# First attention: GpSimd takes the first maxima earlier, and VectorE finishes the layer norm and writes two groups' rows

## The chip, the cores and the metric

The kernel runs on one core of a Trainium2 chip. The metric is the device time of one execution in microseconds (us), the median of several executions; lower is better. The core's engines each work through a queue of their own in order and meet at semaphores: TensorE (PE, matmuls and transposes), VectorE (DVE), ScalarE (ACT), GpSimd (POOL) and SyncE (SP, which here issues the loads).

## The reference

The input x is 16 x 256 tokens of 128 numbers. Four layers follow one another, each with a cross attention onto a context of 64 tokens and a feed-forward part, each behind a layer norm without weights and with a residual sum. The change touches the first attention alone:

```python
def _layernorm(x, axis=-1, eps=1e-05):
    m = jnp.mean(x, axis=axis, keepdims=True)
    v = jnp.var(x, axis=axis, keepdims=True)
    return (x - m) / jnp.sqrt(v + eps)

# _L0_xattn_ref(x, context, mask, Wq, Wkv, Wo): 2 heads of 64
    q = (x @ Wq).reshape(B, N, H, D).transpose(0, 2, 1, 3)
    kv = (context @ Wkv).reshape(B, M, 2, H, D).transpose(2, 0, 3, 1, 4)
    k, v = (kv[0], kv[1])
    attn = jnp.einsum('bhnd,bhmd->bhnm', q, k) * SCALE
    attn = jnp.where(mask[:, None, :, :], attn, -jnp.inf)
    attn = jax.nn.softmax(attn, axis=-1)
    out = jnp.einsum('bhnm,bhmd->bhnd', attn, v)
    out = out.transpose(0, 2, 1, 3).reshape(B, N, C)
    return out @ Wo

    x = x + _L0_xattn_ref(_layernorm(x, axis=-1), ctx_1024, mask_BxSxS2_bf1, ...)
    x = x + _L0_ffn_ref(_layernorm(x, axis=-1), ...)      # quantised: needs maxima over all tokens
```

## The kernel before

The 4096 tokens stay in SBUF as 32 tiles of 128 tokens (X), and the work goes in eight groups of four tiles (512 tokens). All engines' queues are written out by hand, one function for each engine and stage: `att0_pe`, `att0_act`, `att0_dve` and `att0_pool` are the first attention. Nothing else sets the order; a semaphore count in front of an instruction is its only tie to the others.

One group g passes through these steps, named as in the code:

- **Rows** (`normalise` on VectorE, L325, or `norm` on GpSimd, L1180): four instructions write (x - mean) * rstd into `hrow`, which has two places, for even and odd groups. They need the layer norm of their tiles.
- **T(g)** on TensorE (L336) transposes the rows, and ScalarE copies them out (`take_turned`, L341).
- **Q(g)** (L935) is the query product; `takeQ` on ScalarE (L1046, L1049) copies it twice, in bf16 and in f32.
- **MX(g)** (L945, L947) forms the scores in bf16 with the mask added; `mx(g)` on VectorE (L1097) takes each row's negated maximum.
- **less_max(g)** on GpSimd (L1171) adds the negated maximum to the mask.
- **ST(g)** (L960, L962) forms the scores transposed, mask and maximum included. It also waits for the values, since its first use of PSUM bank 3 comes behind V(3), which ScalarE's `values(3)` (L1038) must have copied out. `exp(g)` (L1055) is its exponential.
- **PV(g)** (L972) multiplies by the values, **over(g)** on VectorE (L1105, L1109) divides by the sums, **TO(g)** (L983) transposes, `take_out` (L1061) copies, **O(g)** (L991) is the output product, and `add` (L1115) adds it to X. `tail_stats` (L357, L360) takes the statistics for the next part.

TensorE's order in iteration i is ST(i), Q(i+2), MX(i+1), PV(i), O(i-1), T(i+3), TO(i). Ahead of the loop stand K, V, T(0) to T(2), Q(0), Q(1) and MX(0). In three of the iterations VectorE also quantises the weights of the feed-forward part (`f0_weights_dve`, L1202 to L1208).

The layer norm of x has two parts: tiles 0 to 11 (groups 0 to 2), and tiles 12 to 31, which arrive with a later load. Each part is statistics on VectorE (`first_stats`, L1120), six small instructions (`ln_var_dve`, L224 to L232), a logarithm and an exponential on ScalarE (`ln_finish_act`, L307 and L311), and four small instructions on VectorE (`ln_rstd_dve`, L243 to L249).

GpSimd begins by converting the mask (uint8) into bf16 numbers to add, in eight instructions of two groups' half each (L1161).

Of the kernel before, what the change touches and what calls it, by code (L numbers as in the profile page):

```python
# [32 lines left out]
N_GROUPS = N_TILES // 4  # L33
# [45 lines left out]
def build(nc, dram):  # L79
    with ExitStack() as ctx:  # L80
# [111 lines left out]
        def sem(s, name):  # L192
            return S("all_" + name)

        def at(s, name):
            return sum(count(x, name) for x in SUB[:SUB.index(s)])
# [100 lines left out]
        def ln_finish_dve(dve, s, k=0):  # L297
            ln_var_dve(dve, s, k)
            ln_rstd_dve(dve, s, k)

        def ln_finish_act(act, s, k=0):

            lo, hi = ln_parts(s)[k]
            if s in ("a0", "a1") and k == 0:
                act.preload_act_table_set("natural_log_exp_and_others")
            act.wait_ge(sem(s, "var"), at(s, "var") + k + 1)
            act.activation(lnw[:, 5, lo:hi], lnw[:, 4, lo:hi], ACT.Ln).then_inc(S("all_lnv"), 1)  # L307
            act.wait_ge(S("all_lnv"), at(s, "var") + k + 1)
            if s == "f2" and k == 1:
                act.activation(late_y, lnw[:, 5, lo:hi], ACT.Exp, scale=-0.5)  # L310
            act.activation(lnw[:, 6, lo:hi], lnw[:, 5, lo:hi], ACT.Exp, scale=-0.5).then_inc(sem(s, "std"), 1)  # L311
# [713 lines left out]
        def att0_act(act):  # L1025
            s = "a0"

            def keys(i):
                act.wait_ge(hs("k_ps"), i + 1)
                for h in range(2):  # L1030
                    act.activation(kbd[:, 8 * i:8 * i + 8, h * SK:(h + 1) * SK],
                                   bank(3 + i).rearrange("p (b k) -> p b k", k=SK), ACT.Copy,
                                   scale=W["kmask64"][:, h:h + 1]).then_inc(hs("k"), 1)

            def values(i):
                act.wait_ge(hs("v_ps"), i + 1)
                for h in range(2):
                    act.activation(vw0[:, 4 * i:4 * i + 4, h, 0:64],  # L1038
                                   bank(5 + i if i < 3 else 3).rearrange("p (b n) -> p b n", b=4)[:, :, h * 64:(h + 1) * 64],
                                   ACT.Copy, scale=W["kmask64"][:, h:h + 1]).then_inc(hs("v"), 1)  # L1040

            def takeQ(g):
                act.wait_ge(hs("q_ps"), g + 1)
                if g >= 2:
                    act.wait_ge(hs("mx_ps"), g - 1)
                act.activation(q16_0[g % 2], bank(1), ACT.Copy).then_inc(hs("q16"), 1)  # L1046
                if g >= 3:
                    act.wait_ge(hs("st_ps"), g - 2)
                act.activation(qT0[g % 3], bank(1), ACT.Copy).then_inc(hs("qT"), 1)  # L1049

            def exp(g):
                act.wait_ge(hs("st_ps"), g + 1)
                if g >= 2:
                    act.wait_ge(hs("pv"), g - 1)
                act.activation(pt0[g % 2], bank(3), ACT.Exp, scale=64 ** -0.5).then_inc(hs("pt"), 1)  # L1055

            def take_out(g):
                act.wait_ge(hs("to"), g + 1)
                if g >= 2:
                    act.wait_ge(hs("o_ps"), g - 1)  # L1060
                act.activation(oT0[g % 2], bank(4), ACT.Copy).then_inc(hs("oT"), 1)  # L1061

            keys(0)
            keys(1)
            values(0)
            values(1)
            take_turned(act, s, 0, 0)
            takeQ(0)
            values(2)
            take_turned(act, s, 1, 1)  # L1070
            takeQ(1)
            values(3)
            take_turned(act, s, 2, 0)
            for i in range(N_GROUPS):
                exp(i)
                if i + 2 < N_GROUPS:
                    takeQ(i + 2)
                if i == 0:
                    ln_finish_act(act, s, 1)
                if i + 3 < N_GROUPS:  # L1080
                    take_turned(act, s, i + 3, (i + 3) % 2)
                take_out(i)
            f0_weights_act(act)

        def att0_dve(dve, nxt):
            s = "a0"
            dve.sem_inc(sem(s, "res"), 1)

            def keys16(i):
                dve.wait_ge(hs("k"), 2 * i + 2)  # L1090
                dve.tensor_copy(kbd16[:, 8 * i:8 * i + 8, :], kbd[:, 8 * i:8 * i + 8, :]).then_inc(hs("kb"), 1)

            def mx(g):
                dve.wait_ge(hs("mx_ps"), g + 1)
                if g >= 2:
                    dve.wait_ge(hs("kv"), g - 1)
                dve.tensor_reduce(nm0[g % 2], bank(2).rearrange("p (h k) -> p h k", k=SK), AX.X, ALU.max,  # L1097
                                  negate=True).then_inc(hs("mx"), 1)

            def over(g):  # L1100

                dve.wait_ge(hs("pv"), g + 1)
                both = psum[:, 5:7, 0:260].rearrange("p c (t n) -> p c t n", n=65)
                rz = rz0[g % 2].rearrange("p (c t) -> p c t", c=2)
                dve.reciprocal(rz, both[:, :, :, 64]).then_inc(hs("rz"), 1)  # L1105
                dve.wait_ge(hs("rz"), g + 1)
                if g >= 2:
                    dve.wait_ge(hs("to"), g - 1)
                dve.tensor_tensor(ow0[g % 2].rearrange("p (c t n) -> p c t n", c=2, t=4), both[:, :, :, 0:64],  # L1109
                                  rz.unsqueeze(3).to_broadcast([P, 2, 4, 64]), ALU.mult).then_inc(hs("ow"), 1)  # L1110

            def add(g):
                dve.wait_ge(hs("o_ps"), g + 1)
                xg = X[:, 4 * g:4 * g + 4, :]
                dve.tensor_tensor(xg, xg, bank(7).rearrange("p (t n) -> p t n", t=GT), ALU.add)\  # L1115
                    .then_inc(sem(s, "res"), 1)

            def first_stats(lo, hi):
                for t in range(lo, hi):
                    dve.bn_stats(stats[:, t, :], X[:, t, :]).then_inc(S("bn0"), 1)  # L1120

            normalise(dve, s, 0, 0)
            keys16(0)
            normalise(dve, s, 1, 1)
            dve.wait_ge(S("ld_x"), 32)
            first_stats(LN0, LN0 + 8)
            mx(0)
            normalise(dve, s, 2, 0)
            keys16(1)
            first_stats(LN0 + 8, N_TILES)  # L1130
            mx(1)
            dve.wait_ge(S("bn0"), N_TILES)
            dve.sem_inc(sem(s, "stats"), 1)
            ln_finish_dve(dve, s, 1)
            for i in range(N_GROUPS):
                if i and i + 1 < N_GROUPS:
                    mx(i + 1)
                over(i)
                if i:
                    add(i - 1)  # L1140
                    tail_stats(dve, s, i - 1, False)
                if 3 <= i < 6:
                    f0_weights_dve(dve, i - 3)
            rows_dve(dve)
            add(N_GROUPS - 1)
            tail_stats(dve, s, N_GROUPS - 1, False)
            stats_done(dve, s, nxt)
            dve.sem_inc(S("f0_go"), 1)

        def att0_pool(pool):  # L1150
# [5 lines left out]
                .then_inc(S("f3_pad"), 1)  # L1156
            pool.tensor_copy(vw0[:, :, :, 64], W["kmask64"].unsqueeze(1).to_broadcast([P, B, 2])).then_inc(hs("ones"), 1)
            pool.wait_ge(S("ld_mask"), 16)
            for c in range(4):
                for h in range(2):  # L1160
                    pool.tensor_scalar(m16[:, 8 * c:8 * c + 8, h * SK:(h + 1) * SK],  # L1161
                                       mask_u8[:, 8 * c * SK:8 * (c + 1) * SK].rearrange("p (t k) -> p t k", k=SK),
                                       1.0, MASKED, ALU.subtract, ALU.mult).then_inc(hs("mask"), 1)
# [9 lines left out]
                                   nm0[g % 2].unsqueeze(2).to_broadcast([P, 8, SK]), ALU.add).then_inc(hs("kv"), 1)  # L1173

            def norm(g):
                if g == 3:
                    pool.wait_ge(sem(s, "ln"), 2 * LN_STEPS)
                pool.wait_ge(sem(s, "turned"), at(s, "turned") + g + 1)
                for t in range(GT):
                    ins = pool.tensor_scalar(hrow[:, g % 2, t * P:(t + 1) * P], X[:, 4 * g + t, :],  # L1180
                                             mean[:, 4 * g + t:4 * g + t + 1], rstd[:, 4 * g + t:4 * g + t + 1],
                                             ALU.subtract, ALU.mult)
                ins.then_inc(sem(s, "normed"), 1)

            for g in range(N_GROUPS):
                less_max(g)
                if g + 3 < N_GROUPS:
                    norm(g + 3)
# [1775 lines left out]
```

## Time and profile before

| | |
|---|---|
| median of 3 runs | 1173.81 us (1173.71 to 1174.62) |
| profiled execution | 1166.1 us |
| its span | 1164.3 us |
| mean granted TensorE clock | 0.915 |
| TensorE busy | 937.1 us (80%) |
| VectorE busy | 831.0 us (71%) |
| ScalarE busy | 647.7 us (56%) |
| GpSimd busy | 470.9 us (40%) |

The span runs from the first to the last recorded instruction. The profiled execution took 1.8 us more than its span. It is also 7.7 us shorter than the median of the runs without a profile. The first attention lies in the first 84 us of the span.

### The profile page before, as it was taken

What the parts mean: (1) busy time and instruction counts of PE and PEld (TensorE: products, weight loads), DVE (VectorE), ACT (ScalarE), POOL (GpSimd) and SP (SyncE); (2) the same over time, 40 slices, a digit from 0 to 9 for tenths busy, and PEclk for the clock granted to TensorE, in tenths of its full rate; (3) what the DMA queues carried; (4) which work ended last, traced back from release to release, by engine and by line L of the source; (5) the groups of instructions that cost most, each with busy time, mean ns of one, the idle gap of its engine ahead of it and who ended that gap; (6) DMA issues with size and microseconds to landing.
All of it is one profiled execution on the core that took longest, in us unless ns stands there. A gap on an engine that the chain in (4) does not pass through costs nothing.

```text
span 1164.3 us, 21022 instructions
## 1 busy us (share of the span) xinstructions
PE 937.1 (80%) x7158; PEld 629.4 (54%) x7158; DVE 831.0 (71%) x2070; ACT 647.7 (56%) x1143; POOL 470.9 (40%) x454
## 2 busy tenths in 40 slices
PE   4877820378997999689858999998988987957997
PEld 2663310364545677345434766665654545536896
DVE  5596689876887675467787999999857886622443
ACT  3423567956653345556547878775635655213554
POOL 6610000001220001435368999999311224473555
PEclk9998975588999999899987999999878998987999
DMA  8000000028000000000000000000000000024431
GB/s 288 1 1 1 0 1 0 0 71 273 2 1 1 1 1 2 1 2 1 2 1 1 1 0 0 0 0 1 1 1 1 2 2 1 24 105 116 113 104 34
DMA packets 24233, 33.76 MB, mean 29 GB/s; under 512 B 3484, under 2 KB 20389, under 8 KB 23888
## 3 DMA queue, kind: packets, MB, share of 16 engines
q1 hardware_dynamic: 20720, 26.20, 7.4%
q0 software_dynamic: 3424, 6.38, 1.6%
q8 instruction: 55, 0.90, 0.3%
q14 instruction: 34, 0.28, 0.1%
HBM read 18.34 MB, written 15.98 MB: 29 GB/s over the span
## 4 chain that ended last, share of the span: by engine, by line
PE 33%; DVE 28%; issue 9%; ACT 5%; POOL 3%; DVEq 0%; DMA 0%; POOLq 0%; ACTq 0%; SPq 0%
DVE hq L845 7%; DVE big L850 7%; PE psum L619 5%; PE psum L2523 5%; PE psum L1591 3%; POOL rows L2393 3%; ACT psum L2034 2%; DVE big L2182 2%; PE psum L2539 2%; PE psum L573 2%; PE psum L1608 2%; DVE big L854 2%; DVE psum L1839 1%; DVE tmp L1827 1%; DVE psum L1827 1%
## 5 line engine op out<-in xcount | busy, mean ns | idle before, releaser
L845 DVE TENSOR_REDUCE hq<-psum 128x16 f32<-128x1024 f32 x96 | 114.4, 1220 | 81.2 <-PE psum L573 44.2
L2105 POOL TENSOR_TENSOR big<-big 128x512 f32<-128x512 f32 x128 | 128.7, 1050 | 7.0 <-ACT big L1867 7.0
L2182 DVE SCALAR_TENSOR_TENSOR big<-big,tmp,psum 128x512 f32<-128x512 f32 x128 | 90.4, 744 | 7.6 <-ACT psum L2034 4.7
L2034 ACT ACTIVATE psum<-big,tmp 128x512 f32<-128x512 f32 x128 | 84.9, 686 | 19.3 <-DVE big L2182 16.7
L735 ACT ACTIVATE big<-psum 128x1024 f32<-128x1024 f32 x64 | 62.0, 1021 | 54.5 <-PE psum L603 54.5
L850 DVE RECIPROCAL big<-psum 128x256 f32<-128x256 f32 x48 | 84.0, 1750 | 5.6 <-PE psum L619 5.4
L2710 DVE SCALAR_TENSOR_TENSOR big<-psum,big 128x128 f32<-128x128 f32 x118 | 36.0, 347 | 72.5 <-issue 44.2
L483 POOL TENSOR_TENSOR big<-big,w_const 128x256 f32<-128x256 f32 x32 | 23.3, 728 | 150.3 <-PE psum L619 143.2
L2115 POOL TENSOR_TENSOR big<-big 128x1024 f32<-128x1024 f32 x32 | 75.4, 2366 | 15.8 <-DVE big L2182 15.8
L1505 PE MATMUL psum<-f_downT,tmp 128*128 128x128 f32 x192 | 25.7, 300 | 68.0 <-DVE tmp L1388 68.0
L2403 POOL DMA_INDIRECT out<-big x59 | 57.9, 982 | 50.5 <-issue 30.3
L619 PE MATMUL psum<-big 128*32 128x256 f32 x768 | 52.3, 388 | 26.0 <-DVE big L854 23.9
L1274 DVE TENSOR_REDUCE amax<-big 128x1 f32<-128x1536 f32 x32 | 55.9, 1748 | 22.5 <-ACT big L1414 22.5
L599 PE MATMUL psum<-hq,big 32*128 32x256 f32 x768 | 65.5, 428 | 6.1 <-DVE hq L845 5.9
L341 ACT ACTIVATE hT<-psum 128x512 f32<-128x512 f32 x56 | 33.3, 595 | 61.5 <-PE psum L336 61.5
L2523 PE MATMUL psum<-tmp,big 128*128 x236 | 63.1, 391 | 0.0
L1505 PEld LDWEIGHTS psum<-f_downT,tmp 128*128 128x128 f32 x192 | 25.3, 216 | 68.8 <-DVE tmp L1388 68.3
L1247 POOL PARTITION_ALL_REDUCE qs<-qs x4 | 1.5, 371 | 145.8 <-DVEq L1227 132.2
L491 POOL TENSOR_TENSOR big<-big,w_a 128x256 f32<-128x256 f32 x16 | 11.6, 728 | 119.3 <-ACT big L707 119.3
L336 PE MATMUL psum<-w_const,hrow 128*128 128x128 f32 x224 | 37.8, 295 | 24.5 <-DVE hrow L1298 10.7
L483 POOL TENSOR_TENSOR big<-w_f,w_const 128x256 f32<-128x256 f32 x16 | 12.6, 792 | 108.3 <-PE psum L619 85.4
L619 PE MATMUL psum<-big,w_const 128*32 128x256 f32 x768 | 52.2, 389 | 0.0
(334 smaller groups left out, 2621.4 us busy)
## 6 DMA issues: line engine op xcount, KB each, us to landing
rows<-pad SPq DMA_DIRECT2D x1, 7670.0 KB, 33.0
big<-rows SPq DMA_DIRECT2D x59, 130.0 KB
tmp<-in_pack_f SPq DMA_DIRECT2D x1, 2050.5 KB, 9.7
w_f<-in_pack_f SPq DMA_DIRECT2D x1, 1280.0 KB, 12.6
tmp<-in_pack_once SPq DMA_DIRECT2D x1, 960.0 KB, 7.1
out<-big POOLq DMA_INDIRECT x59
X<-in_x SPq DMA_DIRECT2D x1, 768.0 KB, 5.6
w_a<-in_pack_a SPq DMA_DIRECT2D x3, 256.0 KB, 8.0
```

The source lines that it names most:

```text
L599: pe.matmul(bank(1 + r)[:, 256 * e:256 * e + 256], L.kbd[rows, b, e * P:(e + 1) * P], L.qT[b % L.ahead][rows, :], start=True, stop=False)
L619: ins = pe.matmul(bank(6)[32 * r:32 * r + 32, 256 * which:256 * which + 256], w, L.pt[b % 2][:, (2 * r + e) * 256:(2 * r + e + 1) * 256], ...
L735: act.activation(L.pt[b % 2][:, 1024 * half:1024 * half + 1024], psum[:, 1 + 2 * half:3 + 2 * half, :].rearrange("p c n -> p (c n)"), ACT.Exp,
L845: dve.tensor_reduce(nm, psum[:, 1 + 2 * t:3 + 2 * t, :].rearrange("p c (r l k) -> p (c r) l k", r=2, k=SK), AX.X, ALU.max, negate=True).th ...
L850: dve.reciprocal(L.rz, bank(6)[:, 256:512]).then_inc(hs("rz"), 1)
L1274: dve.tensor_reduce(amax[:, i, g:g + 1], A[:, g, :], AX.X, ALU.max, apply_absolute_value=True).then_inc(S("f0_am"), 1)
L2034: act.activation(bank(EX_BANK + h % 2), ssum[t][:, h * 512:(h + 1) * 512], ACT.Exp, bias=shift2[:, t * NH2 + h:t * NH2 + h + 1]).then_inc( ...
L2105: ins = pool.tensor_tensor(ssum[t][:, h * 512:(h + 1) * 512].rearrange("p (i j) -> p i j", i=ROWS2), st[:, 0, h, 0:ROWS2].unsqueeze(2).to_ ...
L2115: pool.tensor_tensor(ew[t][:, 0:left], ew[t][:, 0:left], ew[t][:, NFOLD * 512:], ALU.add)\
L2182: dve.scalar_tensor_tensor(out=ew[t][:, blk], in0=ssum[t][:, blk], scalar=best2[:, t, h, 7:8], in1=bank(EX_BANK + h % 2), op0=ALU.is_ge, o ...
L2403: pool.indirect_dma_start(dram["out"], bass.IndirectOffsetOnAxis(slot3[j % RS][:, ID3:ID3 + 1].bitcast(U32), 0), out3[j % RS], None, bound ...
L2523: ins = pe.matmul(bank(2 + j % 2)[:, 2 * P * k:2 * P * (k + 1)], hTb[j % 3], W["f3_w"][:, ds(weights_at(j, k), 2 * P)], start=True, stop=True)
```

## The change

- GpSimd: the eight mask conversions are cut into a helper `masks(lo, hi)`, and `less_max(0)` stands behind the fifth of them, `less_max(1)` behind the seventh.
- GpSimd no longer writes the rows of groups 3 and 4. VectorE does, with `normalise`. GpSimd's first `norm` is that of group 5, which also waits until VectorE's rows are counted.
- VectorE: the second part of the layer norm stands right behind its statistics, ahead of `mx(1)`; behind it come the rows of group 3, `mx(1)`, and the rows of group 4.
- ScalarE: the logarithm and the exponential of the second part stand ahead of `takeQ(2)`, not behind it.

```diff
@@ att0_act
             for i in range(N_GROUPS):
                 exp(i)
+                if i == 0:
+                    ln_finish_act(act, s, 1)
                 if i + 2 < N_GROUPS:
                     takeQ(i + 2)
-                if i == 0:
-                    ln_finish_act(act, s, 1)
@@ att0_dve
             first_stats(LN0 + 8, N_TILES)
-            mx(1)
             dve.wait_ge(S("bn0"), N_TILES)
             dve.sem_inc(sem(s, "stats"), 1)
             ln_finish_dve(dve, s, 1)
+            normalise(dve, s, 3, 1)
+            mx(1)
+            normalise(dve, s, 4, 0)
@@ att0_pool
-            for c in range(4):
-                for h in range(2):
+
+            def masks(lo, hi):
+
+                for i in range(lo, hi):
+                    c, h = divmod(i, 2)
                     pool.tensor_scalar(m16[:, 8 * c:8 * c + 8, h * SK:(h + 1) * SK],
...
             def norm(g):
-                if g == 3:
+                if g == 5:
                     pool.wait_ge(sem(s, "ln"), 2 * LN_STEPS)
+                    pool.wait_ge(sem(s, "normed"), at(s, "normed") + 5)
...
-            for g in range(N_GROUPS):
+            masks(0, 5)
+            less_max(0)
+            masks(5, 7)
+            less_max(1)
+            masks(7, 8)
+            for g in range(2, N_GROUPS):
                 less_max(g)
                 if g + 3 < N_GROUPS:
                     norm(g + 3)
```

GpSimd's queue in the first attention, before. L1161 is a mask conversion, L1171 is `less_max`, and four of L1180 are one group's rows:

```order
L1161 TENSOR_SCALAR big<-mask_u 128x8x64 x8
L1171 TENSOR_TENSOR big<-big 128x512
L1180 TENSOR_SCALAR hrow<-X,lnw 128x128 x4
L1171 TENSOR_TENSOR big<-big 128x512
L1180 TENSOR_SCALAR hrow<-X,lnw 128x128 x4
L1171 TENSOR_TENSOR big<-big 128x512
```

The same place of the changed kernel, where the conversions have line L1166, `less_max` L1176 and the rows L1186:

```order
L1166 TENSOR_SCALAR big<-mask_u 128x8x64 [waits ld_mask]
L1166 TENSOR_SCALAR big<-mask_u 128x8x64 x4
L1176 TENSOR_TENSOR big<-big 128x512 [waits att_mask,att_mx]
L1166 TENSOR_SCALAR big<-mask_u 128x8x64 x2
L1176 TENSOR_TENSOR big<-big 128x512 [waits att_mx]
L1166 TENSOR_SCALAR big<-mask_u 128x8x64
L1176 TENSOR_TENSOR big<-big 128x512 [waits att_mask,att_st_ps,att_mx]
L1186 TENSOR_SCALAR hrow<-X,lnw 128x128 [waits all_turned,all_normed,all_ln]
```

Two groups' rows have gone, the first `less_max` stands ahead of three conversions, and the second ahead of one.

VectorE's queue from the last of the first statistics (L1120), before. L1097 is `mx(1)` and L1105 begins `over(0)`:

```order
L1120 BN_STATS stats<-X 128x6 x12
L1097 TENSOR_REDUCE big<-psum 128x8 [waits att_mx_ps]
L224 TENSOR_TENSOR lnw<-stats 128x20 [waits bn0,all_stats]
...
L249 SCALAR_TENSOR_TENSOR lnw<-lnw 128x20 [waits all_ln]
L1105 RECIPROCAL big<-psum 128x8 [waits att_pv,all_ln]
L1109 TENSOR_TENSOR big<-psum,big 128x512 [waits att_rz]
```

The same place of the changed kernel:

```order
L1120 BN_STATS stats<-X 128x6 x12
L224 TENSOR_TENSOR lnw<-stats 128x20 [waits bn0,all_stats]
...
L249 SCALAR_TENSOR_TENSOR lnw<-lnw 128x20 [waits all_ln]
L325 TENSOR_SCALAR hrow<-X,lnw 128x128 [waits all_turned,all_ln]
L325 TENSOR_SCALAR hrow<-X,lnw 128x128 x3
L1097 TENSOR_REDUCE big<-psum 128x8 [waits att_mx_ps]
L325 TENSOR_SCALAR hrow<-X,lnw 128x128 [waits all_turned]
L325 TENSOR_SCALAR hrow<-X,lnw 128x128 x3
L1105 RECIPROCAL big<-psum 128x8 [waits att_pv]
```

`mx(1)` has gone behind the layer norm and the rows of group 3, and `over(0)` behind the rows of group 4 (L325). TensorE's queue is unchanged.

## Rows read from the trace of the kernel before

**Rows 1.** The page, part 4: the chain that ended last, by engine.

```profile
PE 33%; DVE 28%; issue 9%; ACT 5%; POOL 3%; DVEq 0%; DMA 0%; POOLq 0%; ACTq 0%; SPq 0%
```

**Rows 2.** Timeline, TensorE: start, duration, engine, line, operation, tiles, count [idle before, releaser].

```profile
26.92 1.22 PE L960 MATMUL psum<-big 128*128 128x256 f32 x2 [4.47 <-POOL big L1171]
...
37.24 1.11 PE L336 MATMUL psum<-w_const,hrow 128*128 128x128 f32 x4 [5.11 <-POOL hrow L1180]
38.15 1.06 PE L983 MATMUL psum<-w_const,big 128*128 128x128 f32 x4
...
44.38 0.60 PE L983 MATMUL psum<-w_const,big 128*128 128x128 f32 x4
44.82 0.60 PE L960 MATMUL psum<-big 128*128 128x256 f32 x2
...
47.33 1.11 PE L972 MATMUL psum<-big 128*128 128x130 f32 x8
...
50.04 0.60 PE L960 MATMUL psum<-big 128*128 128x256 f32 x2
```

**Rows 3.** Timeline, GpSimd, the first 40 us.

```profile
9.51 16.23 POOL L1161 TENSOR_SCALAR big<-mask_u 128x512 bf16<-128x512 uint8 x8 [1.15 <-DMA mask_u<-in_mask]
25.82 1.04 POOL L1171 TENSOR_TENSOR big<-big 128x512 bf16<-128x512 bf16 x1
34.06 3.12 POOL L1180 TENSOR_SCALAR hrow<-X,lnw 128x128 f32<-128x128 f32 x4 [7.19 <-DVE lnw L249]
```

**Rows 4.** Timeline, ScalarE, around the first scores and in the steady part.

```profile
21.91 0.84 ACT L1038 ACTIVATE big<-psum,w_const 128x256 f32<-128x256 f32 x2
...
29.57 0.60 ACT L1055 ACTIVATE big<-psum 128x512 f32<-128x512 f32 x1 [6.33 <-PE psum L962]
...
46.17 0.60 ACT L1055 ACTIVATE big<-psum 128x512 f32<-128x512 f32 x1 [0.50 <-PE psum L962]
```

**Rows 5.** Timeline, VectorE, from the third group's rows to the first division.

```profile
19.28 1.40 DVE L325 TENSOR_SCALAR hrow<-X,lnw 128x128 f32<-128x128 f32 x4
...
21.20 2.41 DVE L1120 BATCH_NORM_STATS2 stats<-X 128x6 f32<-128x128 f32 x12
31.21 0.69 DVE L1097 TENSOR_REDUCE big<-psum 128x8 f32<-128x512 f32 x1 [7.61 <-PE psum L947]
31.82 0.18 DVE L224 TENSOR_TENSOR lnw<-stats 128x20 f32<-128x20 f32 x1
...
33.05 0.18 DVE L243 TENSOR_TENSOR lnw<-lnw 128x20 f32<-128x20 f32 x1 [0.54 <-ACT lnw L311]
...
33.98 0.21 DVE L1105 RECIPROCAL big<-psum 128x8 f32<-128x8 f32 x1
34.22 0.69 DVE L1109 TENSOR_TENSOR big<-psum,big 128x512 f32<-128x512 f32 x1
```

**Rows 6.** Windows: stretch, length, each engine's busy time (count), granted clock, DMA share, GB/s.

```profile
24.00:26.00 2.00, 0.00 (x0) 0.00 (x0) 0.00 (x0) 0.00 (x0) 1.92 (x2) 1.00 0.93 389
26.00:28.00 2.00, 1.08 (x3) 0.72 (x4) 0.00 (x0) 0.00 (x0) 0.87 (x1) 0.64 0.18 70
...
36.00:38.00 2.00, 0.76 (x4) 0.76 (x5) 0.00 (x0) 0.00 (x0) 2.00 (x3) 0.70 0.00 0
...
40.00:42.00 2.00, 2.00 (x16) 1.28 (x15) 0.00 (x0) 0.74 (x2) 1.29 (x2) 0.94 0.00 0
...
60.00:64.00 4.00, 3.24 (x25) 2.17 (x23) 3.93 (x11) 2.07 (x4) 1.04 (x1) 1.00 0.01 2
...
84.00:88.00 4.00, 3.21 (x17) 3.00 (x16) 2.51 (x16) 0.46 (x2) 0.38 (x1) 0.57 0.01 2
```

**Rows 7.** Timeline, TensorE, behind the last output product of this attention.

```profile
83.19 0.91 PE L2764 MATMUL psum<-w_a,bvmat 128*128 128x128 f32 x6 [2.55 <-DVEq L1148]
```

**Rows 8.** One line's instructions: operation, count, durations in ns (least, median, most).

```profile
L325 DVE TENSOR_SCALAR hrow<-X,lnw x12: 334/453/703, 12.6 to 20.3; 128x128 f32<-128x128 f32 x12
```

**Rows 9.** Timeline, VectorE: the next layer norm's first instruction.

```profile
83.97 0.20 DVE L224 TENSOR_TENSOR lnw<-stats 128x32 f32<-128x32 f32 x1
```

## The prediction, made before the changed kernel had run

> **What bounds the kernel now.** I read the page first. The last chain runs over TensorE and VectorE for 61% of the span, GpSimd has 3% [rows 1], so GpSimd matters only where the others stand still for it. I then read TensorE's timeline of the first 50 us for gaps. There are two. ST(0) starts at 26.92, released by GpSimd's `less_max(0)`, after 4.47 us idle, so T(2) ahead of it ended at 22.45. Behind PV(0) TensorE is idle again for 5.11 us, until T(3) at 37.24, which waits for group 3's rows from GpSimd [rows 2]. From ST(2) on it has no gap: ST(2) to ST(3) is 44.82 to 50.04, so 5.22 us a group, bound by TensorE [rows 2]. Where VectorE quantises the weights, it is the bound: 3.93 us busy of the 4 from 60 to 64 [rows 6]. At 83.97 the next layer norm begins [rows 9]. Each stage behind needs the one ahead, and the only other outside dates are the loads, which are over early: the DMA share is 0.18 at 26 to 28 us and 0.00 behind it [rows 6]. So whatever ST(2) gains, the end should gain. The question is when ST(2) starts; before it is 44.82.
>
> GpSimd's timeline shows both gaps' causes. Eight conversions take 9.51 to 25.74, then `less_max(0)` 1.04. Then GpSimd idles 7.19 us for the layer norm, and the rows take 3.12 [rows 3]. The layer norm's second part starts at 31.82 although its statistics end at 23.61, since `mx(1)` stands ahead and waits 7.61 us for MX(1), which is behind ST(0) on TensorE [rows 5].
>
> **First gap: ST(0).** Five conversions at 16.23 / 8 = 2.03 us end at 9.51 + 10.1 = 19.7, and with 1.04 `less_max(0)` is done at 20.7. `mx(0)`, which it needs, stands ahead of the rows that VectorE starts at 19.28 [rows 5], so it is no later than the fifth conversion. ST(0) is then released by something else: `values(3)` on ScalarE ends at 21.91 + 0.84 = 22.75 [rows 4]. I put ST(0) at 22.82 instead of 26.92. That is 4.10 us. The two conversions behind it end at 20.7 + 4.06 = 24.8 and wait for nobody.
>
> ST(0) also runs faster. In the stretch 24 to 26 us, with TensorE idle, the granted clock is still 1.00 (2.4 GHz). In 26 to 28 it is 0.64 on average, so it fell to 0.50 (1.2 GHz) at about 26.6, and ST(0) runs at that [rows 6]. At full clock ST(i) to `exp(i)` is 44.82 to 46.17, 1.35 us, against 26.92 to 29.57, 2.65, at half [rows 2, 4]. So `exp(0)` starts at 24.17 and ends at 24.77. Before it was 29.57 to 30.17.
>
> **Second gap: T(3) and TO(0).** VectorE goes on from 23.61 with `ln_var`. Before, it took from 31.82 until the wait of 0.54 ahead of L243 at 33.05 began, 0.69 us, so it is ready at 24.3. ScalarE has the logarithm behind `exp(0)` and starts it at 24.77; with the 0.54 that the two functions cost VectorE [rows 5], L243 starts at 25.3. From L243 to the next part's first instruction is 33.05 to 33.98, 0.93: `normalise(3)` starts at 26.25. On ScalarE, `takeQ(2)` comes about 0.5 us later for the move; its copies are next needed by MX(2) and ST(2), far off.
>
> The nearest row for one group's rows on VectorE is 1.40 us for the four at 19.28 [rows 5]. I take it for both groups; by the least and the median of twelve it would be 4 x 0.334 = 1.3 and 4 x 0.453 = 1.8 [rows 8]. So group 3's rows are there at 27.65 and T(3) can start. `mx(1)` (0.69, of which some 0.6 before the next can start) ends at 28.3, the rows of group 4 at 29.7. `over(0)` from its start to its end is 33.98 to 34.91, 0.93, so 30.6. TO(0) starts at 30.65, not 38.15. This is the new last wait. PV ends 3.62 us behind the start of its ST (44.82 to 47.33 + 1.11), so PV(0) ends at 26.4, and TensorE's gaps are now about 1.3 us ahead of T(3) and, T(3) being 0.5 long, 2.4 us between T(3) and TO(0). The eight row instructions add 2.8 us to VectorE, and what is queued behind them is `over(0)`, for which TO(0) and with it all of TensorE waits. That is the price of the move, and it is inside the sum. GpSimd gives 2 x 3.12 us back, most of it idle time anyway.
>
> Who else could be late? `less_max(1)` runs 28.3 to 29.4, ST(1) needs it at 31. The last conversion ends at 31.4. `less_max(2)` waits for `mx(2)`, which follows MX(2), right ahead of PV(1): 2.51 us behind ST(1) (44.82 to 47.33 [rows 2]) and 0.69 for itself, so 34.3. `norm(5)` then ends at 34.3 + 1.04 + 3.12 = 38.5, and T(5) stands 0.9 us ahead of ST(3) at 41.5, so at 40.6. All are hidden, with 1.6, 2.9 and 2.1 us to spare.
>
> **The sum.** At full clock TO(0) takes 0.44 (44.38 to 44.82) [rows 2], ST(1) starts at 31.1 and ST(2) 5.22 later at 36.3. Before: 44.82. Gain 8.5 us.
>
> **The clock.** Less is left if the granted clock falls in the two new gaps. The trace has a fall after a shorter idle time than the two large ones: TensorE idles 2.55 us ahead of L2764 and works again from 83.19, and yet the clock of 84 to 88 is 0.57 [rows 6, 7]. The new gaps are 1.3 and 2.4 us with one 0.5 us transposition between. I choose the fall. How long half clock then lasted is in the means of two stretches: 0.70 in 36 to 38 is a fall at 36.8, and 0.94 in 40 to 42 a return at 40.25 [rows 6], 3.4 us. Work at half clock takes about twice as long (TO(0) lasts 1.06 at 38.15 against 0.60 at 44.38, with its fixed start [rows 2]), so if it falls just ahead of TO(0), 1.7 us of TensorE's work is lost, and if some of it passes in the gap, 1.2. I take 1.4. Gain 8.5 - 1.4 = 7.1 us.
>
> On the profiled execution's own time, 1166.1 - 7.1 = 1159.0 us. The runs' median is 7.7 us above that execution, in which nothing here tells why; I carry the difference over: 1173.8 - 7.1 = **1166.7 us**.
>
> **Rivals.**
> Clock stays full through the gaps: gain 8.5, 1165.3 us. For it: with ST(0) to PV(0) at full speed just before, neither new gap is as long as the 2.55 us ahead of L2764. Against it: the fall at 84 us.
>
> VectorE's rows wait for GpSimd. The mechanism would be that `normalise(4)`, which starts in the same moment as `less_max(1)`, waits for it (1.04) and, losing once more, for the last conversion (1.92). `over(0)` and all behind it come up to 3.0 later: gain 7.1 - 3.0 = 4.1, 1169.7 us. Against it: the twelve row instructions of groups 0 to 2 ran beside conversions that went on without a break, and the longest took 0.703 us [rows 3, 8]. The Trainium skill, SBUF — State Buffer, section on who interferes with whom, says just this: a VectorE tensor_scalar in a two-port mode and a GpSimd instruction lock each other out, and the second to issue blocks fully until the first is done. By that rule instructions among those twelve should have stood for up to a whole conversion, and the time would be this rival's 1169.7. None did, so the trace does not bear it out here.
>
> Hidden anyway: something behind takes the gain back, for instance the weights' load or a date in the next part. The loads are over by 28 us [rows 6], so I know of no such date. 1173.8 us.
>
> Slower: the clock stays at half when the steady part begins. A group there is TensorE work without a gap; were its steps to double nearly all, 5.22 would become about 9.4 us (estimated as 5.22 x 1.8, from TO's 1.06 against 0.60), 4.2 more for each group. Two groups use the gain up; over four groups it is 7.1 - 16.8 = 9.7 us slower, 1183.5 us. For it: at 84 us the clock fell under a working TensorE. Against it: behind both large gaps it came back, the second time after 3.4 us, once gap-free work ran [rows 6].
>
> That the change doesn't do what it says I rule out: the queues show `less_max(0)` behind the fifth conversion.
>
> **How the numbers follow.** Forecast (clock falls, gain about 7): 0.50; its own range is 1166.3 to 1168, from the 1.7 and 1.2 of the clock and 0.8 for slower rows. Clock stays: 0.27. Rows wait for GpSimd: 0.08. A smaller gain of 2 to 5 from a wait I haven't seen: 0.07. Hidden: 0.03. Slower: 0.05. This kernel's measurement tells about 0.2% (2.3 us) from no change. So faster 0.91, same 0.04, slower 0.05. Range: below, the full gain 8.5, with 1.7 us more if the runs' own two clock dips cost more than the profiled one's, 1163.5; above, the GpSimd rival, 1170.0.
>
> **What would show it.** In the changed profile: ST(0) (L960) at 22.8, released by ScalarE's L1038 and not by GpSimd; layer norm L243 at 25.3; L325 eight more times, of which the last ends near 29.7; TO(0) (L983) at 30.6 released by VectorE's L1109; ST(2) at 37.7 (36.3 with a full clock); the next layer norm at about 77 instead of 83.97. The windows from 30 to 34 us tell whether the clock fell. The forecast is wrong if `over(0)` ends past 32, if GpSimd's L1176 releases ST(1), or if the first attention is 7 us shorter and the total is not.

## The result, and the profile after

The changed kernel took 1170.16 us (median of 7 runs, 1169.31 to 1172.08), the kernel before, run beside it, 1174.26. The ratio is 0.9957, 95% interval 0.9937 to 0.9978, so by the ratio it is 5.0 us faster (2.6 to 7.4); the two medians lie 4.1 us apart. The forecast was 7.1 us, 1166.7; the median lies 0.2 us above the range that was given, with a kernel before that ran 0.5 us longer than in the runs at hand then. Two later repetitions gave ratios of 0.9959 and 0.9976 (below). So the direction was right and the size too large by 2 to 4 us.

TensorE's timeline of the profile after, to be laid beside [rows 2]. This execution ran 0.63 us ahead of the first from the start: T(2) starts at 21.16 instead of 21.79. That is not the change's work: e4 below, whose code is the same up to there, has T(2) at 21.88.

```profile
21.16 0.66 PE L336 MATMUL psum<-w_const,hrow 128*128 128x128 f32 x4
22.25 0.67 PE L960 MATMUL psum<-big 128*128 128x256 f32 x2 [0.43 <-ACT big L1038]
...
27.52 0.66 PE L336 MATMUL psum<-w_const,hrow 128*128 128x128 f32 x4 [1.58 <-DVE hrow L325]
31.14 1.11 PE L983 MATMUL psum<-w_const,big 128*128 128x128 f32 x4 [2.96 <-DVE big L1109]
32.05 1.06 PE L960 MATMUL psum<-big 128*128 128x256 f32 x2
...
39.01 0.60 PE L960 MATMUL psum<-big 128*128 128x256 f32 x2
```

These rows show the two gaps and what ends them. ST(0) is released by ScalarE's values after 0.43 us, no longer by GpSimd after 4.47. T(3) comes 9.7 us earlier by the clock of the trace. But TO(0) waits 2.96 us for VectorE's division, TO(0) to ST(1) takes 0.91 us, which is half clock, and ST(1) to ST(2) takes 6.96 instead of the 5.22 of a full-clock group. With the 0.63 us added, TO(0) stands at 31.77 (forecast 30.65) and ST(2) at 39.64 (forecast 37.7). The gain at ST(2) is 44.82 - 39.64 = 5.2 us.

VectorE's timeline, to be laid beside [rows 5], shows why TO(0) waited:

```profile
18.63 2.47 DVE L325 TENSOR_SCALAR hrow<-X,lnw 128x128 f32<-128x128 f32 x4
...
21.63 2.40 DVE L1120 BATCH_NORM_STATS2 stats<-X 128x6 f32<-128x128 f32 x12
24.19 0.19 DVE L224 TENSOR_TENSOR lnw<-stats 128x20 f32<-128x20 f32 x1 [0.15 <-DVEq L1132]
...
25.42 0.18 DVE L243 TENSOR_TENSOR lnw<-lnw 128x20 f32<-128x20 f32 x1 [0.54 <-ACT lnw L311]
...
26.35 1.12 DVE L325 TENSOR_SCALAR hrow<-X,lnw 128x128 f32<-128x128 f32 x4
27.38 0.69 DVE L1097 TENSOR_REDUCE big<-psum 128x8 f32<-128x512 f32 x1
27.98 2.26 DVE L325 TENSOR_SCALAR hrow<-X,lnw 128x128 f32<-128x128 f32 x4
30.17 0.19 DVE L1105 RECIPROCAL big<-psum 128x8 f32<-128x8 f32 x1
```

One group's rows take 1.12 us (group 3) and 2.26 (group 4), and group 2's, whose code the change does not touch, 2.47 instead of 1.40. GpSimd's timeline beside it:

```profile
19.29 1.04 POOL L1176 TENSOR_TENSOR big<-big 128x512 bf16<-128x512 bf16 x1
20.42 3.93 POOL L1166 TENSOR_SCALAR big<-mask_u 128x512 bf16<-128x512 uint8 x2
28.15 1.07 POOL L1176 TENSOR_TENSOR big<-big 128x512 bf16<-128x512 bf16 x1 [3.81 <-DVE big L1097]
29.30 1.92 POOL L1166 TENSOR_SCALAR big<-mask_u 128x512 bf16<-128x512 uint8 x1
```

Both slow groups have a `less_max` beside them, at 19.29 and at 28.15, and the conversion that follows it. Looked at one by one, the rows hold an instruction that lasts far longer than the 0.703 us of [rows 8] (columns as there):

```profile
L325 DVE TENSOR_SCALAR hrow<-X,lnw x20: 332/472/1140, 12.3 to 29.9; 128x128 f32<-128x128 f32 x20
```

The windows, to be laid beside [rows 6], show the clock:

```profile
28.00:30.00 2.00, 0.18 (x2) 0.00 (x0) 2.00 (x5) 0.60 (x1) 1.76 (x2) 0.69 0.03 8
30.00:32.00 2.00, 0.86 (x4) 0.86 (x5) 1.05 (x3) 0.00 (x0) 1.22 (x1) 0.50 0.00 0
32.00:34.00 2.00, 2.00 (x8) 1.34 (x7) 0.00 (x0) 0.60 (x1) 0.00 (x0) 0.50 0.00 0
34.00:36.00 2.00, 2.00 (x8) 0.96 (x7) 0.00 (x0) 0.60 (x1) 0.00 (x0) 0.60 0.00 0
```

A mean of 0.69 is a fall from full clock (2.4 GHz) to half (1.2 GHz) at 28.8, and one of 0.60 a return at 35.6. It stayed at half for 6.8 us, 4.5 of them with TensorE at work, not for 3.4.

The next layer norm begins at 78.16 instead of 83.97 [rows 9]: what was gained at ST(2), 5.8 us by the trace's clock (5.2 without the earlier start), came through the rest of the first attention whole.

```profile
78.16 0.20 DVE L224 TENSOR_TENSOR lnw<-stats 128x32 f32<-128x32 f32 x1
```

Yet this execution took 1169.6 us, 3.5 more than the profiled one of before. In the last stage both VectorE and ScalarE stand still for some 12 us, with no releaser that the profile knows ("remote"), as the waits of the kernel after say (engine, line, releaser: total, times, longest):

```profile
DVE big L2655 <- remote: 15.1, 2, 11.5
ACT big L2559 <- remote: 12.2, 1, 12.2
```

### The profile page after: what moved, and what is told of

Read it like the earlier page. It is cut to its first block, busy times and chain, and to the rows that moved or that the text cites. A ratio compares the mean times of both kernels' runs of the same rounds, so it can differ in the third digit from the quotient of the medians.

```text
span 1167.8 us, 21022 instructions
## 1 busy us (share of the span) xinstructions
PE 939.7 (80%) x7158; PEld 630.9 (54%) x7158; DVE 836.0 (72%) x2078; ACT 647.1 (55%) x1143; POOL 464.6 (40%) x446
## 4 chain that ended last, share of the span: by engine, by line
PE 35%; DVE 29%; issue 8%; ACT 5%; another core or an unknown queue 1%; POOL 1%; DVEq 1%; DMA 0%; POOLq 0%; ACTq 0%; SPq 0%
DVE big L850 7%; DVE hq L845 7%; PE psum L619 5%; PE psum L2534 5%; PE psum L1602 3%; ACT psum L2045 2%; DVE big L2193 2%; PE psum L2550 2%; PE psum L573 2%; PE psum L1619 2%; DVE big L854 2%; DVE psum L1850 1%; DVE tmp L1838 1%; DVE psum L1838 1%; PE psum L2436 1%
## 5 line engine op out<-in xcount | busy, mean ns | idle before, releaser
L1972 PEld LDWEIGHTS psum<-w_const,big 128*128 128x128 f32 x384 | 47.3, 196 | 8.6 <-issue 8.6
```

## The experiments

Each was timed in rounds beside the kernel before, on the same chip: e1 to e4 on one chip, e5 to e8 on another, e9 and e10 later on that second one. The kernel before had a median of 1167 to 1168 us in all three sets, about 6 less than in the first comparison. Runs of different sets are compared by their ratios.

| run | median us | ratio, 95% interval | gain us |
|---|---|---|---|
| e1, before again | 1167.13 | 0.9997 (0.9983 to 1.0011) | 0.4 |
| e2, first maxima early alone | 1163.59 | 0.9959 (0.9943 to 0.9975) | 4.8 |
| e3, rows and layer norm on VectorE alone | 1164.38 | 0.9971 (0.9958 to 0.9984) | 3.4 |
| e4, division ahead of group 4's rows | 1158.42 | 0.9917 (0.9901 to 0.9934) | 9.7 |
| e5, after again | 1162.76 | 0.9959 (0.9946 to 0.9973) | 4.8 |
| e6, both groups' rows ahead of mx(1) | 1160.90 | 0.9944 (0.993 to 0.9957) | 6.5 |
| e7, gap filled | 1159.26 | 0.993 (0.9917 to 0.9944) | 8.2 |
| e8, e4 with less_max kept apart | 1156.92 | 0.991 (0.9895 to 0.9925) | 10.5 |
| e9, before a third time | 1167.64 | 1.0004 (0.999 to 1.0017) | -0.5 |
| e10, after a third time | 1163.83 | 0.9976 (0.9965 to 0.9988) | 2.8 |

The gain is one minus the ratio, times the median of the kernel before beside it (1167.98, 1167.81 or 1166.86).

### Is the stop in the last stage the change's? (e1, e5, e9, e10)

The kernels are the two of the comparison, unchanged.

> The kernel before, unchanged, profiled once more. In the changed kernel's profile VectorE and ScalarE stand still for 11.5 and 12.2 us at about 1018 to 1030 us, with no releaser in the profile; the first profile of the kernel before has no such stop and is 7.7 us shorter than its timed runs. Theory A (the stop belongs to this program's usual executions, and the first profile was an exception): this profile takes 1173 to 1175 us and shows a stop of some 8 us in the last stage. Rival B (the changed kernel brings the stop): no stop here, a profiled execution of about 1166 us again. The ratio is 1.000 by both.

> The changed kernel, unchanged, beside the others of this call. Theory: it gains at ST(2) what its first profile showed, 5.2 us once the earlier start is taken off, so a ratio of 0.9955; TO(0) follows T(3) by 3.6 us with the clock at half from then on. The stop of 11.5 us of VectorE and ScalarE in the last stage of its first profile: by theory A (part of any execution now and then, of this program or of the other) it is absent or elsewhere in this profile; by rival B (a part of the changed kernel) it is there again at about 1018 us.

> The kernel before, profiled a third time. The executions timed beside the changed kernel's first profile had a median of 1174.3 us, those beside the later runs 1168. If this is the slower set again, theory A expects a stop of VectorE and ScalarE of 7 to 12 us in the last stage of this profile, at a time of about 1174 us; at a time of about 1167 us no such stop, as in the two profiles so far. Rival B expects no stop at either time.

> The changed kernel, profiled a third time beside the kernel before. In either set it is 5 us faster than that one; a stop in the last stage is in both kernels' profiles or in neither by theory A. Rows of group 4 again 2.2 to 2.3 us, TO(0) 3.6 us behind T(3).

No profile of the four has a wait on "remote". The spans are 1165.5 and 1166.4 us before, 1157.0 and 1158.2 after. So rival B has fallen in its strict form: the changed kernel runs without the stop, twice of three profiles. Theory A is not shown either, since no execution of the kernel before with a stop was caught; e1 missed the 1173 to 1175 us that it had been given. The executions that would decide it, at 1174 us, did not come again. What the rows do give is the stop's price. From the first instruction of the last layer norm to the end of the span it is 202.8 us in the profile with the stop, and 195 to 196 in each of e1 to e10. That is 7.5 us, near the 6 to 7 by which both kernels' medians lay higher in the first comparison. A stop in most executions of that comparison, of either kernel, would fit this. It is an argument only, and the first profile of before, with 192.0 us in this stretch, differs from all the others too.

The early part repeats well. In e5 T(2) starts at 21.27 and TO(0) at 31.27, group 4's rows take 2.27 us, and ST(2) starts at 39.21 against 45.19 in e1. In e10 it is 39.88 against 45.82 in e9. The next layer norm comes 5.8, 6.0 and 6.0 us earlier in the three pairs of profiles, of which 0.6, 0.5 and 0.8 are the earlier start (T(2)). The timed runs say 5.0, 4.8 and 2.8.

### The two parts alone (e2, e3)

e2 keeps the rows of groups 3 and 4 on GpSimd:

```diff
-            for c in range(4):
-                for h in range(2):
...
-            for g in range(N_GROUPS):
+            masks(0, 5)
+            less_max(0)
+            masks(5, 8)
+            norm(3)
+            less_max(1)
+            norm(4)
+            for g in range(2, N_GROUPS):
```

> One part alone: less_max(0) behind the fifth mask conversion; conversions six to eight, the rows of groups 3 and 4 on GpSimd and VectorE's and ScalarE's order as before. Theory: ST(0) starts 4.1 us earlier at full clock, and with it MX(1), mx(1), the layer norm and GpSimd's rows of group 3: by the chain MX(1), mx(1), layer norm, 3.1 us of rows, T(3) starts near 31.7 instead of 37.2 and ST(2) about 5.4 us earlier, which is as much as or more than the whole change gave at ST(2) (5.8 us with 0.6 us of it from an earlier start). So a median of 1168.5 to 1170. Rival: the rows on VectorE carry the gain, and this part alone gives 4.1 us or less, 1170 to 1172.

It gained 4.8 us. Its TensorE timeline (T(2) at 22.70, so 0.9 later from the start than in e1):

```profile
23.81 0.67 PE L960 MATMUL psum<-big 128*128 128x256 f32 x2 [0.45 <-ACT big L1038]
...
32.60 1.11 PE L336 MATMUL psum<-w_const,hrow 128*128 128x128 f32 x4 [5.10 <-POOL hrow L1183]
```

ST(0) went as expected, and T(3), less 0.9, came at 31.7. The whole first gap was saved, and the second kept its 5.1 us. ST(2) started at 41.72, which less 0.9 is 4.4 us earlier than in e1, not 5.4. What is missing is the clock's, for ST(1) to ST(2) took 7.36 us where e1 had 5.96. A mean of 0.97 in 30 to 32 us and of 0.82 in 38 to 40 is half clock from 31.9 to 38.7, 6.8 us, where e1 had 3.4 behind the same gap. The whole change gained 5.4 us at ST(2) by e5 against e1, each from its own T(2). So in the trace this part gave four fifths of the whole. The timed runs can't tell the two apart, and 4.8 us (2.9 to 6.7) does not rule out the rival's 4.1 either.

e3 is the changed kernel with all conversions first:

```diff
-            masks(0, 5)
-            less_max(0)
-            masks(5, 7)
-            less_max(1)
-            masks(7, 8)
+            masks(0, 8)
+            less_max(0)
+            less_max(1)
```

> The other part alone: VectorE's and ScalarE's order and the rows of groups 3 and 4 on VectorE as in the change, but all eight mask conversions ahead of less_max(0). Theory: ST(0) stays at 26.9 at half clock, exp(0) at 29.6; the layer norm's logarithm waits for exp(0) and comes at 30.2, so rows of group 3 at 31.7 to 32.8, rows of group 4 with no conversion beside them, over(0) ends near 35.5, TO(0) at 35.6 instead of 38.15: a gain of 2.5 us, median about 1171.7. Rival (the parts do not add up because the gap ahead of TO(0) is the same): no gain, 1174.

It gained 3.4 us (1.9 to 4.9), and TO(0) started at 35.94. The theory stands, and the rival, no gain, fell. Group 4's rows took 1.83 us, with only `less_max(1)` beside them:

```profile
33.21 1.83 DVE L325 TENSOR_SCALAR hrow<-X,lnw 128x128 f32<-128x128 f32 x4
```

At ST(2) the parts gain 4.4 and 1.9 us, 6.3 together, and the whole change 5.4. By the timed runs it is 4.8 and 3.4 against 4.8, each give or take 1.3 to 1.9 us. What is lost between them is in the new gap ahead of TO(0), which the next runs take apart.

### The gap ahead of TO(0) (e4, e6)

e4 changes two places on VectorE:

```diff
             mx(1)
+            over(0)
             normalise(dve, s, 4, 0)
...
-                over(i)
+                if i:
+                    over(i)
```

> The changed kernel with over(0) ahead of group 4's rows on VectorE. Theory (TO(0) at 31.14 waited for over(0), which stood behind rows of 2.26 us, and the clock fell in that gap of 2.96 us): TO(0) starts near 28.9, the gap ahead of it is about 0.5 us, the clock stays full, ST(2) at about 34.3 instead of 39.0: 3.5 to 4.7 us less than the changed kernel, median 1165.5 to 1167. Rival (the clock falls all the same in the gap ahead of T(3)): 2.2 us less, 1168. Rival (the next wait takes its place, less_max(1) or group 4's rows for T(4)): less than 1 us.

It gained 9.7 us, 4.9 more than e5 by the ratios. TO(0) started at 29.49 after a gap of 0.78 us, the granted clock was 1.00 in every stretch from 22 to 38, and ST(2) started at 35.20. In the trace both rivals fell: the clock did not, and the next wait came nowhere near. Group 4's rows are not wanted before T(4) at 34.33, 4.8 us behind TO(0), and they had been put ahead of the one instruction for which TensorE stood still.

e6 leaves the division last but moves both groups' rows ahead of `mx(1)`:

```diff
             normalise(dve, s, 3, 1)
-            mx(1)
             normalise(dve, s, 4, 0)
+            mx(1)
```

> The changed kernel with the rows of group 3 and of group 4 both ahead of mx(1), so that both are written while GpSimd has nothing under way. Theory (group 4's rows took 2.26 us and group 3's 1.12 because GpSimd ran less_max(1) beside the first): both take 1.1 us, over(0) starts 1.1 us earlier and TO(0) with it; 1.1 us less than the changed kernel, or about 2 less where the shorter gap spares clock. Rival (group 4's rows are slow for another reason, their place in SBUF or the load's late tiles): 2.2 us again, no gain.

VectorE's timeline of e6, with both groups in one row:

```profile
26.59 2.14 DVE L325 TENSOR_SCALAR hrow<-X,lnw 128x128 f32<-128x128 f32 x8
28.64 0.69 DVE L1097 TENSOR_REDUCE big<-psum 128x8 f32<-128x512 f32 x1
29.24 0.20 DVE L1105 RECIPROCAL big<-psum 128x8 f32<-128x8 f32 x1
```

Eight instructions take 2.14 us when GpSimd rests, so the same rows of group 4 are about 1.1 and not 2.27. It is GpSimd's work beside them that stretched them, not their place or tiles, and the rival fell. `less_max(1)` alone made them 1.83 (e3), 0.7 more; the other 0.4 came with the conversion that follows it. TO(0) came 1.05 us earlier than in e5 (30.22 against 31.27), but ST(2) only 0.5 (38.68 against 39.21): in both runs the clock's means are 0.76 in 28 to 30 and 0.53 in 34 to 36, so half clock lasted from 29.0 to 35.9 in both, and work that came earlier met more of it. By the ratios e6 gained 1.7 us more than e5, with intervals that overlap.

### What half clock cost (e7)

```diff
                 if i + 3 < N_GROUPS:
                     T(i + 3)
+                if i == 0:
+                    for t in range(20):
+                        pe.transpose(bank(7)[:, (t % 4) * P:(t % 4 + 1) * P], ident, ident)
                 TO(i)
```

> The changed kernel with 20 more transposes of the identity into a PSUM bank that nobody reads, between T(3) and TO(0), some 2.2 us at full clock in a gap of 2.96 us. Theory (the granted clock fell in this gap and half clock cost about 2 us): the clock stays at 1.00 from 28 to 38 us, ST(1) to ST(2) takes 5.22 and not 6.96 us, TO(0) 0.44 and not 0.91, and the kernel is 2.2 us faster than the changed one. Rival (the clock falls whatever fills the gap, or the gap ahead of T(3) is what makes it fall): ST(1) to ST(2) again near 6.9, the same time or, with the fillers in the way of TO(0), up to 1 us more.

TensorE's timeline of e7:

```profile
27.52 0.66 PE L336 MATMUL psum<-w_const,hrow 128*128 128x128 f32 x4 [1.60 <-DVE hrow L325]
28.01 2.35 PE L1020 MATMUL psum<-w_const 128*128 128x128 f32 x20
31.14 0.66 PE L983 MATMUL psum<-w_const,big 128*128 128x128 f32 x4 [0.79 <-DVE big L1112]
31.63 0.60 PE L960 MATMUL psum<-big 128*128 128x256 f32 x2
...
36.85 0.60 PE L960 MATMUL psum<-big 128*128 128x256 f32 x2
```

Its windows, where e5 has 0.76, 0.50, 0.50 and 0.53 in the clock's column:

```profile
28.00:30.00 2.00, 2.00 (x21) 2.00 (x20) 2.00 (x5) 0.60 (x1) 1.77 (x2) 1.00 0.00 0
30.00:32.00 2.00, 1.21 (x10) 0.90 (x9) 1.05 (x3) 0.17 (x1) 1.22 (x1) 1.00 0.00 0
32.00:34.00 2.00, 2.00 (x16) 1.22 (x14) 0.00 (x0) 1.13 (x3) 0.00 (x0) 1.00 0.00 0
34.00:36.00 2.00, 2.00 (x23) 2.00 (x21) 1.37 (x3) 0.98 (x2) 0.89 (x1) 1.00 0.00 0
```

TO(0) starts at the same time as in the first profile after, 31.14, behind the same rows of 2.27 us. With 20 transposes whose result nobody reads, the clock does not fall, TO(0) to ST(1) is 0.49 instead of 0.91, and ST(1) to ST(2) 5.22 instead of 6.96. That is 2.2 us at ST(2), as expected, and the clock's part in the first attention is shown. By the ratios e7 gained 3.4 us more than e5, and the intervals do not overlap; the 1.2 us beyond ST(2)'s are not traced. Over the whole program e7's mean granted clock was 0.914 to 0.917, e5's 0.910 to 0.914.

### less_max kept away from the rows (e8)

On top of e4's edit:

```diff
-            masks(0, 5)
+            masks(0, 6)
             less_max(0)
-            masks(5, 7)
+            masks(6, 8)
             less_max(1)
-            masks(7, 8)
```

> over(0) ahead of group 4's rows as in the run before it, and GpSimd's order changed so that less_max(0) comes behind six conversions and less_max(1) behind all eight. Theory (less_max(0) beside group 2's rows makes these 2.3 us instead of 1.4, which delays the statistics and the layer norm by about 0.6): group 2's rows take 1.4 to 1.6 us, the layer norm starts 0.6 us earlier, ST(0) is released at the same time, since six conversions and less_max(0) end at about 22.8; 0.5 us less than the run with over(0) first alone. Rival (ST(0) now waits for less_max(0)): same time or up to 0.7 us more.

VectorE's timeline of e8:

```profile
19.31 1.27 DVE L325 TENSOR_SCALAR hrow<-X,lnw 128x128 f32<-128x128 f32 x4
...
23.66 0.19 DVE L224 TENSOR_TENSOR lnw<-stats 128x20 f32<-128x20 f32 x1 [0.15 <-DVEq L1132]
...
25.34 0.18 DVE L243 TENSOR_TENSOR lnw<-lnw 128x20 f32<-128x20 f32 x1 [0.98 <-ACT lnw L311]
```

Group 2's rows are 1.27 us beside a conversion; in e4, beside `less_max(0)`, they are 2.27. The layer norm starts 1.05 us earlier than in e4 (24.71), of which 0.6 reaches L243, for the logarithm now waits behind `exp(0)` (0.98 us instead of 0.54). ST(0) is at 22.93 as in e4, and ST(2) at 34.63 instead of 35.20. The theory stands in the trace. In the time, a ratio of 0.9910 against 0.9917, the step is too small to be told. This is the fastest version, 10.5 us below the kernel before and 5.8 below the changed one.

## Why the prediction was right, and where its size was off

**The first gap** was read rightly: ST(0) released by ScalarE's values, `exp(0)` at full clock, the conversions behind it in nobody's way. This part of the edit alone (e2) gained 4.4 us at ST(2), and 4.8 in the timed runs.

**The rows on VectorE** were mis-sized, and this is the step that failed first. I took 1.40 us for each group, with 1.8 as the upper bound, from twelve instructions that ran beside conversions [rows 5, 8]. Group 3's took 1.12, group 4's 2.26: 0.6 us more for the pair. The same contention had a second effect that I did not name at all. `less_max(0)`, moved up, now lies beside the rows of group 2. They went from 1.40 to 2.47 us, and with them L243, behind the statistics and the layer norm's first instructions, from my 25.3 to 26.05 (25.42 + 0.63). Both together make TO(0) 1.1 us late.

I had weighed this as a rival, at 0.08, and set it aside, since beside GpSimd's conversions, 1.92 us long, no row instruction took longer than 0.703 us. That is true, but of conversions only. Beside a `less_max` of 1.04 us, one row instruction lasts 1.07 to 1.14 us instead of 0.34. So the rival's mechanism did come about, in the order that it gave: `less_max(1)` cost group 4's rows 0.7 us and the last conversion 0.4, 1.1 in place of its 3.0.

The Trainium skill, SBUF — State Buffer, section on who interferes with whom, says that of a VectorE tensor_scalar in a two-port mode and a GpSimd instruction the second to issue blocks fully. The measurement agrees for GpSimd's tensor_tensor (28.15 to 29.22), with the row instruction that started just behind it and ended 0.08 us after it. It disagrees for the uint8 conversion. In e9 a conversion that began at 19.45 was under way when group 2's rows started at 19.93. These took 1.10 us, as if alone; it was the conversion, the second of the two in this row, that grew from 1.92 to 2.65 us (the timeline from 19 us on):

```profile
17.45 4.65 POOL L1161 TENSOR_SCALAR big<-mask_u 128x512 bf16<-128x512 uint8 x2
19.93 1.10 DVE L325 TENSOR_SCALAR hrow<-X,lnw 128x128 f32<-128x128 f32 x4
```

I carried the row of one GpSimd instruction over to another kind, and dismissed the rule with it.

**The clock** fell, as I chose. Its cost was mis-sized: I took one stay at half clock of 3.4 us, cost 1.4; it stayed for 6.8, and TO(0) and the group behind ST(1) lost 0.5 + 1.7 = 2.2 us. e7 gives just that back at ST(2). A length read once was not enough here. The kernel before has both: its second gap, of 5.1 us, was followed by 3.4 us at half clock in its first profile and in e1, and by 6.8 in e9, in whose rows 0.71 is a fall at 34.8 and 0.58 a return at 41.7:

```profile
34.00:36.00 2.00, 0.00 (x0) 0.00 (x0) 1.26 (x4) 0.00 (x0) 1.39 (x2) 0.71 0.00 0
40.00:42.00 2.00, 2.00 (x9) 1.35 (x8) 0.00 (x0) 0.45 (x2) 1.84 (x3) 0.58 0.00 0
```

So the forecast took the shorter of two lengths as the only one. The first profile after, e5, e6 and e10 all have 6.8 us. 1.1 us from the rows and 0.8 from the clock are the 1.9 us between the forecast and the measured ST(2), which leaves a gain there of 5.2 us against 7.1. Two of the three comparisons say 5.0 and 4.8; the third, 2.8, goes with neither.

**GpSimd's slack** was right: ST(1), ST(2) and T(5) did not wait for it. The rival "hidden anyway" fell, since the next layer norm came 5.8 us earlier. The slower rival, half clock through the steady part, fell too.

**What stays open.** The third comparison says 2.8 us (1.4 to 4.1), although its profile has the same 6.0 us at the next layer norm as the others. The single executions there go with TensorE's mean granted clock. The changed kernel took 1160.0 us at 0.912, 1161.3 and 1162.2 at 0.911, and 1163.6 to 1165.0 at 0.909 to 0.910. The kernel before took 1164.6 to 1168.7 at 0.912 to 0.915, and 1166.5 to 1170.5 at 0.907 to 0.910. So the profiled execution with the 6.0 us is the fastest of its eight, and likewise in e5, where it took 1158.8 us at 0.914 and the others 1161.7 to 1164.4 at 0.910 to 0.911. The share of half clock over the whole program differs from one execution to the next. In e10 the changed kernel was at 0.912 or less in all eight, the kernel before at 0.912 or more in 15 of 22, which by itself may take back part of the gain. What sets it was not traced. Nor is the cause of the stop of 12 us settled, or why the first comparison ran 6 us slower for both kernels.

## What to carry to other kernels

When work is moved to an engine that TensorE waits for, put it behind the instruction that TensorE waits for, not ahead: group 4's rows stood ahead of `over(0)` and were wanted 4.8 us later than its result, and changing the two places doubled the gain. When an instruction of GpSimd is moved, look at what now runs beside it on VectorE, the unchanged instructions too, and take a price for the pair only from a row with that same pair. A gap that shrinks but still lets the clock fall costs twice, once for the wait and once for the work at half clock behind it; compare the time until the clock returns, and read it from more than one execution.

## What the runs showed of the hardware

A VectorE tensor_scalar of 128x128 f32 between SBUF tiles takes about 0.26 us from start to start with GpSimd at rest (2.14 us for eight, of which the last lasts 0.34), and four take 1.12. Beside GpSimd's conversion of uint8 to bf16 four take 1.10 to 1.62 us, and the conversion itself grows from 1.92 to as much as 2.65. Beside GpSimd's tensor_tensor of 128x512 bf16 (1.04 us) one of the four lasts 1.07 to 1.14, in every profile where the tensor_tensor starts while they run. The four then take 1.83 with nothing behind the tensor_tensor (e3), and 2.26 to 2.48 with a conversion behind it.

The granted clock fell in a stretch in which TensorE had idled 1.6 us, transposed for 0.5 and idled 2.96 more, and stayed at half for 6.8 us, although TensorE worked for the last 4.5 of them without a pause. With gaps of 1.4 and 0.8 us around the same transposition (e4) it did not fall. The stay of 6.8 us is not peculiar to two gaps: behind a single gap of 5.1 us it was 3.4 in two profiles (before, e1) and 6.8 in two others (e2, e9).
